# Causal mask of the transposed scores: TensorE's mask product, or GpSimd's select on the probabilities

## The reference

```python
kv = latent_kv @ Wkv_expand.T
k, v = jnp.split(kv, 2, axis=-1)
...
scores = jnp.einsum('bhqd,bhkd->bhqk', qh, kh) * inv_sqrt_d
causal = jnp.tril(jnp.ones((sq, sk), dtype=bool))
scores = jnp.where(causal, scores, jnp.finfo(scores.dtype).min)
attn = jax.nn.softmax(scores, axis=-1)
out = jnp.einsum('bhqk,bhkd->bhqd', attn, vh)
```

## Time and profile before

| | |
|---|---|
| median of 3 runs | 1258.27 us (1255.56 to 1265.9) |
| profiled execution, its own time | 1262.43 us |
| its span | 1260.3 us |
| mean granted TensorE clock | 0.981 |
| PE busy | 1181.7 us (94%), 6016 matmuls |
| DVE busy | 696.4 us (55%) |
| ACT busy | 455.0 us (36%) |
| POOL busy | 448.1 us (36%) |
| cross-attention in the span | about 518 to 890 us |

### The profile page before, as it was taken

How to read it: one execution, slowest core, us unless ns; L and a number is a source line. 1 busy time by engine, 2 the same in 40 slices (tenths; PEclk the granted TensorE clock), 3 DMA queues, 4 the chain that set the end, 5 groups by cost and what they waited for, 6 DMA issues and landing times.

```text
span 1260.3 us, 15629 instructions
## 1 busy us (share of the span) xinstructions
PE 1181.7 (94%) x6016; PEld 780.8 (62%) x6016; DVE 696.4 (55%) x990; ACT 455.0 (36%) x758; POOL 448.1 (36%) x392
## 2 busy tenths in 40 slices
PE   3979999999999799899999999989999999999998
PEld 2745566465556444555555555545788788887886
DVE  6566657666676567566667667554553423333212
ACT  4135533544464356435335344444132111111110
POOL 6235632643454645624425347446200001001000
PEclk9989999999999899999999999888999999999999
DMA  5833333352243423425524625520131000000000
GB/s 200 257 111 84 84 85 84 99 146 61 73 123 106 128 80 121 115 84 154 134 79 131 173 75 156 166 59 18 42 101 34 34 1 0 34 0 0 34 1 34
DMA packets 42757, 110.27 MB, mean 87 GB/s; under 512 B 5569, under 2 KB 10689, under 8 KB 36545
## 3 DMA queue, kind: packets, MB, share of 16 engines
q1 hardware_dynamic: 39888, 101.99, 28.0%
q0 software_dynamic: 2080, 6.82, 1.7%
q10 hardware_dynamic: 720, 0.54, 0.1%
HBM read 71.58 MB, written 37.75 MB: 87 GB/s over the span
## 4 chain that ended last, share of the span: by engine, by line
PE 77%; DVE 10%; POOL 5%; issue 3%; ACT 3%; DMA 0%; DVEq 0%; ACTq 0%; SPq 0%; POOLq 0%
PE PS L793 16%; PE PS L794 15%; PE PS L795 15%; PE PS L920 10%; PE PS L905 8%; PE PS L883 7%; DVE m_cols L1129 6%; POOL P_sum L594 2%; PE PS L915 2%; POOL oTL L584 1%; PE PS L807 1%; DVE PT L1089 1%; PE PS L886 1%; PE PS L908 1%; ACT PT L720 1%
## 5 line engine op out<-in xcount | busy, mean ns | idle before, releaser
L1129 DVE TENSOR_REDUCE m_cols<-PS 128x1 f32<-128x512 f32 (+3 forms) x432 | 281.3, 668 | 177.1 <-PE PS L883 93.9
L720 ACT ACTIVATE PT<-PS 128x512 f32<-128x512 f32 (+1 forms) x432 | 237.8, 580 | 172.0 <-PE PS L905 79.7
L594 POOL TENSOR_TENSOR P_sum<-PT 128x512 f32<-128x512 f32 x128 | 161.4, 1281 | 375.2 <-ACT PT L720 375.2
L883 PE MATMUL PS<-stackK,stackQ 96*128 96x512 f32 (+3 forms) x512 | 191.7, 410 | 15.3 <-DVE m_cols L1129 13.1
L905 PE MATMUL PS<-stackQ,stackK 100*128 100x512 f32 (+3 forms) x512 | 179.7, 400 | 6.0 <-ACT PT L720 5.4
L1202 DVE CAST hidH<-hid 128x512 fp32r<-128x512 f32 x64 | 30.5, 477 | 223.2 <-ACT hid L765 221.1
L883 PEld LDWEIGHTS PS<-stackK,stackQ 96*128 96x128 f32 x512 | 93.2, 196 | 85.2 <-DVE m_cols L1129 57.6
L765 ACT ACTIVATE hid<-PS,b1c 128x512 f32<-128x512 f32 x64 | 44.0, 687 | 277.7 <-PE PS L795 275.8
L905 PEld LDWEIGHTS PS<-stackQ,stackK 100*128 100x128 f32 x512 | 91.4, 191 | 78.4 <-ACT PT L720 29.9
L1137 DVE RECIPROCAL P_sum<-PS 128x512 f32<-128x512 f32 x32 | 107.4, 3358 | 55.1 <-PE PS L920 55.1
L600 POOL TENSOR_TENSOR P_sum<-P_sum,PT 128x512 f32<-128x512 f32 x96 | 120.4, 1280 | 8.5 <-ACT PT L720 4.5
(11 more groups left out here) (111 smaller groups left out, 1711.0 us busy)
## 6 DMA issues: line engine op xcount, KB each, us to landing
scratch<-stage SPq DMA_DIRECT2D x128, 256.0 KB, 7.5
stackQ<-scratch SPq DMA_DIRECT2D x32, 512.0 KB, 4.7
stackK<-scratch SPq DMA_DIRECT2D x32, 512.0 KB, 7.2
stackQ<-scratch SPq DMA_DIRECT2D x32, 256.0 KB, 5.3
stackK<-scratch SPq DMA_DIRECT2D x32, 256.0 KB, 8.2
PT<-wT SPq DMA_DIRECT2D x3, 1024.0 KB, 9.0
x_res<-x SPq DMA_DIRECT2D x3, 1024.0 KB, 8.5
out<-x_res SPq DMA_DIRECT2D x3, 1024.0 KB, 4.4
```

Of the source, the lines that this page charges most:

```text
L594: pool.tensor_tensor(P_sum[:, h, :], PT[:, h, :], PT[:, 4 + h, :], ALU.add).then_inc(p_added, 1)
L720: nc.scalar.activation(PT[:, slot:slot + heads, q0:SEQ], PS[:, T_BANK + n % 2, 0:heads * width].rearrange("p (h n) -> p h n", h=heads), AC ...
L883: mm = nc.tensor.matmul(dst[:, a, :], stackQ[0:STACK, par, h + a, q * P:(q + 1) * P], stackK[0:STACK, par, h + a, 0:n], start=a == 0, stop ...
L1129: nc.vector.tensor_reduce(m_cols[:, q, STACK + h:STACK + h + heads], PS[:, S_BANK + m % 2, 0:heads * n].rearrange("p (h n) -> p h n", h=he ...
```

## The change

GpSimd's select takes the place of TensorE's mask product. `scores` of a cross unit ends with its last real product. For each key tile, after the four heads' exponentials, GpSimd runs one `affine_select` over the diagonal block of all four heads (128 partitions x 4 x 128 fp32, in PT, in place) and writes zero above the diagonal. Values and additions of a cross unit wait for it (`p_masked`) and no longer for the exponential (`p_ready`). GpSimd's order becomes: select 0, `low_output` of the unit before, select 1, four additions, `low_raw` below place 9, select 2, select 3, two additions, later `low_raw`. `mask_kq` with its memset and its select at the start goes.

```diff
+            def mask_probabilities(u, k):
+
+                pool.wait_ge(p_ready, fills_until(u, k, HPG - 1))
+                slot, q0 = 4 * k % 8, queries(u, k)
+                block = PT[:, slot:slot + HPG, q0:q0 + P]
+                pool.affine_select(out=block, in_=block, compare_op=ALU.is_ge, fill=0.0, base=0,
+                                   pattern=[[0, HPG], [1, P]], channel_multiplier=-1).then_inc(p_masked, 1)
+
             def add_probabilities(u, k, h):
                 heads = ADD_HEADS[layer_of(u)] if k == 2 else 1
-                pool.wait_ge(p_ready, fills_until(u, k, h + heads - 1))
+                if layer_of(u) == CROSS:
+                    pool.wait_ge(p_masked, masks_until(u, k))
+                else:
+                    pool.wait_ge(p_ready, fills_until(u, k, h + heads - 1))
...
                 for n in raws_of(u, 0.0, 3.0):
                     low_raw(n)
+                cross = layer_of(u) == CROSS
+                if cross:
+                    mask_probabilities(u, 0)
+                    low_output(u - 1)
+                    mask_probabilities(u, 1)
                 for h in range(HPG):
-                    if u and h == 2:
+                    if u and h == 2 and not cross:
                         low_output(u - 1)
                     add_probabilities(u, 1, h)
                 for n in raws_of(u, 3.0, 9.0):
                     low_raw(n)
+                if cross:
+                    mask_probabilities(u, 2)
+                    mask_probabilities(u, 3)
                 for h in range(0, HPG, ADD_HEADS[layer_of(u)]):
                     add_probabilities(u, 2, h)
                 for n in raws_of(u, 9.0, 99.0):
...
                 for a in range(heads):
                     mm = nc.tensor.matmul(dst[:, a, :], stackK[0:STACK + HPG, par, h + a, k * P:(k + 1) * P],
-                                          stackQ[0:STACK + HPG, par, h + a, q0:SEQ], start=a == 0, stop=not cross)
-                if cross:
-                    mm = nc.tensor.matmul(dst[:, :, 0:P], identb[:, :],
-                                          mask_kq[:, :].unsqueeze(1).broadcast_to([P, heads, P]), start=False, stop=True)
+                                          stackQ[0:STACK + HPG, par, h + a, q0:SEQ], start=True, stop=True)
                 mm.then_inc(t_full, 1)
...
-                pe.wait_ge(p_ready, fills_until(u, k, HPG - 1))
+                if layer_of(u) == CROSS:
+                    pe.wait_ge(p_masked, masks_until(u, k))
+                else:
+                    pe.wait_ge(p_ready, fills_until(u, k, HPG - 1))
```

More of the change, by code:

```diff
@@ L81, with masks_until @@
 ADD_HEADS = {SELF: 1, CROSS: 2}
+def masks_until(u, k):
+    return KT * (u - FIRST_CROSS) + k + 1
 def adds_before(u):
@@ L99 @@
 FIRST_RAW = 12
-CONSTS = 13
+CONSTS = 11
 CHUNK_PLACES = [(25, (10.0, 12.0)), (26, (10.0, 12.0)), (28, (7.0, 10.0)), (28, (16.0, 20.0)), (29, (10.0, 12.0)),
@@ L284, in decoder_layer @@
         mask_qk = sb("mask_qk", [P, P], BF16)
-        mask_kq = sb("mask_kq", [P, P], BF16)
         stats = sb("stats", [P, KT, 6], F32)
@@ L358, in decoder_layer @@
         p_used = sem("p_used")
+        p_masked = sem("p_masked")
         p_added = sem("p_added")
@@ L530, in _ @@
             pool.memset(mask_qk[:, :], 0.0).then_inc(consts, 1)
-            pool.memset(mask_kq[:, :], 0.0).then_inc(consts, 1)
-            pool.wait_ge(consts, 6)
+            pool.wait_ge(consts, 5)
             pool.affine_select(out=identb[:, :], in_=identb[:, :], compare_op=ALU.not_equal, fill=1.0,
@@ L536, in _ @@
                                base=0, pattern=[[-1, P]], channel_multiplier=1).then_inc(consts, 1)
-            pool.affine_select(out=mask_kq[:, :], in_=mask_kq[:, :], compare_op=ALU.is_ge, fill=MASKED,
-                               base=0, pattern=[[1, P]], channel_multiplier=-1).then_inc(consts, 1)
             def later_consts():
@@ L902, in scores @@
                 dst = PS[:, T_BANK + m % 2, 0:heads * n].rearrange("p (h n) -> p h n", h=heads)
-                cross = layer_of(u) == CROSS
                 for a in range(heads):
                     mm = nc.tensor.matmul(dst[:, a, :], stackK[0:STACK + HPG, par, h + a, k * P:(k + 1) * P],
-                                          stackQ[0:STACK + HPG, par, h + a, q0:SEQ], start=a == 0, stop=not cross)
-                if cross:
-                    mm = nc.tensor.matmul(dst[:, :, 0:P], identb[:, :],
-                                          mask_kq[:, :].unsqueeze(1).broadcast_to([P, heads, P]), start=False, stop=True)
+                                          stackQ[0:STACK + HPG, par, h + a, q0:SEQ], start=True, stop=True)
                 mm.then_inc(t_full, 1)
```

## The result

The changed kernel took 1306.93 us (median of 4 runs, 1302.67 to 1307.55), the kernel before 1259.91 (its three runs and one more on the same chip, 1255.56 to 1265.9). The ratio is 1.037, with a 95% interval of 1.033 to 1.042: slower by 47 us, above the forecast of 1283 and above the range's upper end of 1302. The profiled execution took 1307.08 us, 44.65 more than that of before.

What follows compares the result with a forecast made beforehand. TensorE was taken as the bound, with 77% of the chain that ended last. The terms, 5.3-1.3-3.0+10.5+3.6+6.3+3.5 = +24.9 us on the profiled 1262.43, gave 1287.3; less 4.16 over the median, 1283 was forecast, range 1266 to 1302.

Steps and rivals of the forecast that it cites:

- The chain: Middle units: select 1, four additions, exponential 9 and select 2 delay values 2; 0.9 us a unit, +5.3 for six.
- the walk: Step-by-step timing of middle unit 18 under the new GpSimd order; values 2 starts at 583.97, period 19.4 us.
- The clock in middle units: The sum held no clock loss in middle units; only a rival had it, about 2 us each, +12.
- The 5.33 us behind it don't shrink: Middle units: the fixed order from values 2 to the next unit keeps its 5.33 us, so the unit grows 0.9.
- third rival: Selects cost 1.28 us, 1300 us; or the clock also falls behind waits in middle units, 1295 us; together 22%.
- stretches with half a us of idling keep 1.00: Argument for the clock staying up in first units, which would give 1277 us; that rival had 18%.
- First units: Units 16, 20, 24: later tile +3.5 us each (+10.5) and lower clock 2.1 each (+6.3); unit 28 +3.6.
- a sign of being wrong: In first units, VectorE's tile instruction L1089 ending while GpSimd runs on; 2 to 3 us long would be right.
- VectorE doesn't get through while GpSimd goes from one two-input instruction to the next: First units: GpSimd's run holds VectorE's tile, so the transposes start 3.5 us later in units 16, 20, 24.
- Units 29 and 30: TensorE's own stretch there is long enough to cover GpSimd's work: -0.65 us each, -1.3 together.
- Last units, unit 31: Units 19, 23, 27 gain 1.0 us each, -3.0; unit 31's sums wait for GpSimd's last additions, +3.5.
- The lead: Cross units without mask products have fills ready sooner: 0.6 us by fill 7, 1.0 by the unit's end.

Runs made afterwards that it cites:

- e3: Changed kernel with seven unread bf16 products on TensorE ahead of its wait for select 2, in first and middle units: 1283.90 us, ratio 1.019.
- e14: Changed kernel with unread products on TensorE wherever it idles in cross units 16 to 30: 1274.67 us, ratio 1.009.
- e9: Changed kernel with seven unread bf16 products behind values 2, not ahead of its wait: 1295.83 us, ratio 1.030.
- e1: Kernel before with the mask products taken out and nothing in their place, so its output differs: 1252.41 us, ratio 0.994.
- e2_both: Changed kernel with the mask product kept on TensorE beside the selects: 1297.78 us, ratio 1.030.
- e13: Kernel before with unread products ahead of unit 28's transposes and of fills 2, 4 and 6 in units 29 and 30: 1252.25 us, ratio 0.995.
- e10_best: Kernel before with masks of key tiles 0 and 3 moved to GpSimd, plus unread products where TensorE idles in units 28 to 30: 1252.20 us, ratio 0.994.

## Why the prediction was right in kind and too low

**The chain (right).** One select is 0.637 us, for 0.64 worked out of the earlier trace rows. Values 2 waits on the select. With the clock held (e3, e14) a middle unit is 19.31 to 19.34 us; the walk said 19.4. Six of them cost 4.9 us, for 5.3. By the Trainium skill (GPSIMD Engine Reference, section 3.1) the best case for 512 elements is 769 ns. The trace has 637, and the measurement decides.

**The clock in middle units (the step that failed).** The sum had the clock fall only behind the long waits for the tile, as in unit 28. The walk of unit 18 went on at full clock behind its wait: it took the 5.33 us behind values 2 as they stood ("The 5.33 us behind it don't shrink"). It is not so: behind 1.52 us of waiting the clock was 0.57, and 0.50 a unit later. The six middle units cost 19.5 us, of which 14.5 are the clock (after against e14). The prediction had this as half of its third rival, "about 2 us each, +12", without a share of its own in the sum. What speaks for the cause is shown from three sides: e3 takes it away by filling the wait, e9 has the same products elsewhere and doesn't, and e1 has fewer products, no wait, and clock 1.00.

The Trainium skill (TensorE: Matmul & The Clock Gate, section "A second HAM failure mode: psum-queue depth-cycling") tells of another kernel, a bf16 one, in which TensorE idles briefly but often between groups of matmuls, so that its clock gate falls and rises again, and throughput is lost each time. The trace agrees, with 21.00 to 22.67 us for units that take 19.33 at full clock. I read "stretches with half a us of idling keep 1.00" as if all between 0.5 and 2.1 us were safe. The trace of before has waits of lengths between, which I hadn't looked up, and they speak both ways. Two of 1.02 us in the self-attention, at 200.56 and 314.93, have 1.00 in the 8 us behind them. One of 1.33 us at 87.53, the fifth of 0.5 us or more within 10 us, has 0.53 behind it. The first of the two:

```profile
200.56 0.63 PE L807 MATMUL PS<-ident,PT 128*128 128x128 f32 x4 [1.02 <-DVE PT L1089]
```

```profile
201.00:209.00 8.00, 7.92 (x40) 6.08 (x42) 5.95 (x10) 0.71 (x2) 0.00 (x0) 1.00 0.26 96
```

Nor does the length alone decide in e2_both (1.09 us each time, the clock down in three units of six). What else decides, no run shows.

**First units (the sum nearly right, its terms not).** Forecast were 5.6 us each, 3.5 for the tile and 2.1 for the clock; measured 4.0, 4.3 and 5.05. The clock's part is 6.4 for the three (after against e14), for 6.3. The tile's part is 2.3 each (e14 against before). The mechanism is there: the tile waited 5.71 us for GpSimd and ended 0.28 after GpSimd's run of L613. But it took 1.36 us in all three units, where 2 to 3 were forecast, and wasn't held through the next `low_raw` too, which followed without a gap and itself took 1.45 us for 1.28. This is what the prediction had named as a sign of being wrong, L1089 (here L1109) ending while GpSimd runs on. So "VectorE doesn't get through while GpSimd goes from one two-input instruction to the next", read from unit 28 alone, is wrong as a rule: here it got through at the end of the additions. The transposes began 17.5 us into the unit, not 19.0, and TensorE waited 1.80 us for them, not 3.5. In unit 28 the tile again took 2.60 us, through the `low_raw` of 1.25, as before, and the unit grew by 2.8, for 3.6. What makes unit 28 differ from the other three stays open; no run tried it.

**Units 29 and 30 (wrong sign).** I took -0.65 each, since TensorE's own stretch would cover the chain. It grew by 1.24 and 1.34. With the clock held in both (e14 18.76, e13 17.32) the chain costs 1.44 each. TensorE's stretch looked long in the trace of before only because part of it ran at the lower clock (17.32 us when held, 20.45 when not). Cover that is made of slow clock isn't cover.

**Last units, unit 31 (right in kind).** With the clock held the last units shrink by 0.77 each, for 1.0; with it falling now and then, by 1.3 in all, for 3.0. Unit 31 and what follows it grew by 3.2, for 3.5, and its sums waited for L613.

**Self-attention (0 forecast, 4.6 measured).** Its instructions are the same in all these kernels, but for constants at the very start. The copy that starts unit 16 lies between 515.5 and 522.2 us in the 16 profiled executions, in both kinds of kernel: 515.5 in e2_both, made from the changed kernel, 522.2 in e10_best, made from the one before. The five that start by 517.3 us have a clock of 1.00 in the 70 us ahead of it, the other eleven 0.93 to 0.95. Of the five, four are among the seven made from the kernel before, and one among the nine made from the changed one; whether the change makes the lower clock more frequent is open. So is how much of the 47 us of the medians this is.

**The gain that was to pay for it.** The lead was put at 1.0 us a unit, 16 in all; e1 shows 0.76 in middle units and 7.6 us in all by the medians. So the exchange was bad even with the clock held: about 19 us of cost, after the gain.

By the sum: 24.9 forecast, 44.8 measured in the profiled executions. Of the 19.9 between them, 14.2 are the middle units, 4.6 the self-attention, 3.9 units 29 and 30, 1.7 the last units, less 3.4 in first units, 0.8 in unit 28 and 0.3 in unit 31.

## What to carry to other kernels

When a change makes TensorE wait in the middle of a dense loop, price the wait twice: once for itself, once for TensorE's work behind it at the lower clock, and put the second into the sum unless the trace has waits of that length, coming as often, with the clock up behind them. Where such a wait can't be removed, a few small products that nobody reads, put ahead of it, can pay: here 23 us of the 47 lost, in twelve of the units, and about 0.5% of the kernel before. Look for short recurring waits in the kernel as it is, too, since a stretch that seems long enough to hide new work may only be slow. Work moved to another engine belongs behind everything that this engine's other readers wait for: follow each of its outputs to all its consumers before choosing the order.

## What the runs showed of the hardware that was not expected

- Waits of about 1.5 us in middle units, in a TensorE that is otherwise busy, came with a granted clock of 0.50 to 0.63 in the stretches of 8 or 9 us shown above. Seven bf16 products in the wait (1.67 us) kept it at 1.00. With 1.09 us of waiting (e2_both) it stayed up in three middle units of six.
- The same fill behind the wait took 3.17 us for 1.67: the lower clock doubled the price of each product, and units 17 and 18 were still 22.92 and 22.10 us long.
- The self-attention of one and the same program text ended between 515.5 and 522.2 us, with a granted clock of 1.00 between 447 and 517 us in one (before) and 0.93 in others (the changed kernel, e10_best). So 6.7 us of a difference between two profiled executions can come from this.
- VectorE's pass over 128x512 in SBUF was held while GpSimd ran its two-input additions and ended 0.28 us after them, in units 16, 20 and 24. In unit 28 it was held through one more of GpSimd's instructions (2.60 us for 1.36). Where GpSimd doesn't run, the pass takes 0.54 us (198.22 in the trace of before).
